# Moving the loads of the spike counts from SP's DMA queue to POOL's in the last stage of a gated attention layer

## The reference

```python
xn = layernorm(x)
# attention by pooling, 16 heads of 64
mixed_q = xn @ Wq + bq
mixed_k = xn @ Wk + bk
q_w = softmax((mixed_q @ Wqa + bqa) * scale, axis=tokens)
pooled_q = sum over tokens of q_w * mixed_q          # one row of 1024
mixed_qk = mixed_k * pooled_q
k_w = softmax((mixed_qk @ Wka + bka) * scale, axis=tokens)
pooled_k = sum over tokens of k_w * mixed_qk         # one row of 1024
s = (pooled_k * mixed_q) @ Wt + bt + mixed_q
# feed-forward with spikes
y = square(relu(xn @ W_fc.T)) @ W_proj.T             # hidden size 4096
cnt = number of spikes of y in 5 steps               # 0 to 5
out = x + s * silu(cnt / 5)
```

## Time and profile before

| what | value |
|---|---|
| median of 2 runs | 1622.05 us (1620.1 to 1624.01) |
| profiled execution | 1621.26 us |
| span of its slowest core (core 5) | 1619.6 us |
| spans of the eight cores | 1595.9 to 1619.6 us |
| granted TensorE clock, mean by core | 0.921 to 0.931 |
| busy: PE, DVE, ACT, POOL | 83%, 45%, 23%, 9% of the span |
| moved by DMA on this core | 174.19 MB, 108 GB/s |

### The profile page before, as it was taken

The page is one execution under the profiler, slowest core; times in us unless marked ns, Lnnn a source line. Parts: engine busy times, 40 slices in busy tenths (PEclk is TensorE's granted clock), DMA queues, the critical chain, the costliest instruction groups (busy, mean ns, idle before and its releaser), DMA issues.

```text
span 1619.6 us, 26631 instructions; the slowest of 8 cores (1595.9 to 1619.6 us)
## 1 busy us (share of the span) xinstructions
PE 1349.4 (83%) x8997; PEld 838.4 (52%) x8997; DVE 727.5 (45%) x1257; ACT 365.5 (23%) x804; POOL 149.9 (9%) x268
## 2 busy tenths in 40 slices
PE   1165599999999999999999999999999076379983
PEld 0032266666666666666666666666666032134431
DVE  3221136546464554645546465464645411244544
ACT  1323322313222131221313223132222000011221
POOL 1334400000000000000000000000022025120000
PEclk9976699999999999999999999999999575589997
DMA  6857701011010111101111010110013937647776
GB/s 184 249 170 243 244 28 60 34 66 45 36 60 33 53 47 47 60 31 55 46 47 59 21 60 34 66 59 21 34 59 101 318 117 217 226 136 235 235 248 219
DMA packets 66559, 174.19 MB, mean 108 GB/s; under 512 B 9671, under 2 KB 10071, under 8 KB 66410
## 3 DMA queue, kind: packets, MB, share of 16 engines
q1 hardware_dynamic: 34234, 77.90, 16.8%
q0 software_dynamic: 13824, 46.21, 8.3%
q10 hardware_dynamic: 18368, 48.37, 7.8%
HBM read 121.99 MB, written 50.46 MB: 106 GB/s over the span
## 4 chain that ended last, share of the span: by engine, by line
PE 69%; DMA 18%; DVE 5%; ACT 3%; issue 2%; SPq 2%; POOL 1%; DVEq 0%; ACTq 0%; POOLq 0%
PE PS L518 26%; PE PS L497 26%; PE PS L402 7%; DMA AM<-cnt_scratch 7%; DMA XF<-WfcT 2%; PE PS L681 2%; DMA XF<-WprojT 2%; DMA AB<-xtm_scratch 2%; PE PS L406 2%; PE PS L816 2%; PE PS L899 1%; SPq L633 1%; DMA OB<-WprojT 1%; DMA SCA<-xn_scratch 1%; ACT YS L527 1%
## 5 line engine op out<-in xcount | busy, mean ns | idle before, releaser
L497 PE MATMUL PS<-SCA,AB 128*128 128x256 bf16 x4096 | 539.9, 276 | 45.6 <-ACT RB L502 45.6
L518 PE MATMUL PS<-AB,AM 128*128 128x512 bf16 x2048 | 543.0, 385 | 6.3 <-ACT YS L527 4.7
L497 PEld LDWEIGHTS PS<-SCA,AB 128*128 128x128 bf16 x4096 | 403.3, 99 | 210.0 <-issue 57.0
L506 DVE TENSOR_TENSOR AM<-RB 128x256 bf16<-128x256 f32 x512 | 225.1, 440 | 554.4 <-PE PS L518 257.3
L502 ACT ACTIVATE RB<-PS 128x256 f32<-128x256 f32 x512 | 196.6, 384 | 761.8 <-PE PS L497 317.0
L518 PEld LDWEIGHTS PS<-AB,AM 128*128 128x128 bf16 x2048 | 189.1, 99 | 165.4 <-issue 26.3
L402 PE MATMUL PS<-SCA,AM 128*128 128x256 bf16 x1024 | 139.6, 280 | 49.7 <-DVE SCA L410 34.6
L552 DVE SCALAR_TENSOR_TENSOR AM<-YS,AM 128x1024 bf16<-128x1024 f32 x128 | 156.4, 1222 | 0.8
L402 PEld LDWEIGHTS PS<-SCA,AM 128*128 128x128 bf16 x1024 | 101.5, 100 | 67.0 <-issue 53.7
L278 POOL CAST AB<-OB 128x512 bf16<-128x512 f32 x55 | 35.9, 654 | 1039.2 <-PE PS L497 1001.3
L899 PE MATMUL PS<-AM,AB 128*128 128x512 bf16 x384 | 91.5, 392 | 3.2 <-DVE OB L926 1.9
(11 more groups left out here) (120 smaller groups left out, 694.9 us busy)
## 6 DMA issues: line engine op xcount, KB each, us to landing
XF<-x SPq DMA_DIRECT2D x64, 512.0 KB, 4.6
xn_scratch<-SCA ACTq DMA_DIRECT2D x16, 512.0 KB, 2.7
xtm_scratch<-SCA ACTq DMA_DIRECT2D x32, 256.0 KB, 3.2
mq_scratch<-SCA ACTq DMA_DIRECT2D x16, 512.0 KB, 2.7
cnt_scratch<-AM ACTq DMA_DIRECT2D x32, 256.0 KB, 3.2
AB<-xtm_scratch SPq DMA_DIRECT2D x32, 256.0 KB, 9.5
AM<-cnt_scratch SPq DMA_DIRECT2D x32, 256.0 KB, 5.2
out<-OB POOLq DMA_DIRECT2D x16, 512.0 KB, 6.3
```

The source lines that it names most:

```text
L497: pl.comp("tensor", lambda te, hb=hb, lt=lt, rh=rh, c=c: te.matmul(hb[:, 0:256], lt, rh, start=(c == 0), stop=(c == 7)), reads=a1keys(c * ...
L506: pl.comp("vector", lambda v, h2=h2, rr=rr: v.tensor_mul(h2, rr, rr), reads=[krr], writes=[("h2", g3)])
L518: pl.comp("tensor", lambda te, yb=yb, lt=lt, rh=rh, j=j: te.matmul(yb[:], lt, rh, start=(j == 0), stop=(j == 31)), reads=[kh2] + a2keys(j ...
```

## The change

`ld_cnt3` issues its DMA from POOL's stream in place of SP's. It has 32 calls: two ahead of the last loop, and one at the end of each of the loop's first 30 tiles. Slots, keys and semaphores are the same.

```diff
         def ld_cnt3(t):
             slot = AM[:, 10240 + (t % 2) * 1024: 10240 + (t % 2) * 1024 + 1024]
             alias = [("spk",)] if t % 2 == 0 else [("spk",), ("h2", 2), ("h2", 3)]
-            pl.dma("sync", f"cr{t % 2}",
+            pl.dma("gpsimd", f"cr{t % 2}",
                    lambda s, slot=slot, t=t: s.dma_start(slot, cnt_d[t]),
                    reads=[("cntd", t)], writes=[("cntr", t % 2)] + alias)
```

## The result

The changed kernel is slower by 0.8%: ratio to the kernel before 1.0082, with a 95% interval of 1.0056 to 1.0108. Of 1622 us that is 13 us, where the prediction had +10 and a range of 1614 to 1660. The median over all its runs is 1639.91 us, the profiled execution took 1636.4 us; its slowest core, core 1, has a span of 1634.5 us. Three of its executions took 1734 to 1824 us with four cores at a clock of 0.79 to 0.87 in place of 0.92, and ratios and intervals here leave such executions out for every kernel.

A forecast was written before the change was run, and what follows sets the result against it. Waits on count loads in the last loop, with neither TensorE nor DMA engines full, were taken to set 10.76 us a pair. +0.64 us over 15 pairs is +10 us: 1621.26 + 10 = 1631 us, range 1614 to 1660.

The forecast's parts named there:

- What bounds the kernel: Last loop: neither TensorE nor DMA is full; waits on count loads set 10.76 us a pair, through two nearly equal loops.
- The even loop as a whole: Last loop, even tiles: 7.2 us from addition to counts landed, plus 4.2, gives 11.4 us a pair against 10.76.
- The issue of the even counts: POOL, behind the even store: counts issued 1.21 us after the addition, against 0.55 on SP, 0.66 us later.
- The landing of the even counts: POOL's queue: store lands 7.1 us after the addition, counts 0.6 behind it at 7.7, less relief 7.2.
- the half microsecond of relief from sharing: SP's queue carries 256 KB less, 1.1 us; half of it, 0.5 us, is credited to POOL's queue.
- The odd load: Odd counts on POOL, nothing ahead: landing in 3.6 us is covered, in 5.2 makes the next even load 0.5 us late; put at nothing.
- The sum: Last loop: +0.64 us a pair over 15 pairs, +10 us, giving 1631 us.
- The early loads: Two count loads ahead of the last loop, on POOL behind mq loads: 21 us wait inside 35 us idle, put at nothing.
- A: Rival: the odd loop was what cost and gets shorter, no change or faster, 1619 or 1595 us; chance 0.18.
- B: Rival: POOL's queue gets the small share, even counts land late, over 2% slower, +47 us, 1668; chance 0.17.
- C: Rival: DMA bandwidth as a whole sets the pace, so the time stays at 1621 to 1623 us; chance 0.13.
- The signs: Profile after: count-load share not below 7%; wrong if additions under 10.6 us, odd landing last, or store doesn't delay counts.

The follow-up runs named there:

- store_sp_nokey: store_sp with no count load from tile 2 on waiting for the load before: ratio to the kernel before 1.0012 (0.9994 to 1.0029).
- nokey_sp: Kernel before, counts still on SP, without the shared key from tile 2 on: no interval, two of four times 1621.75 and 1629.02 us, against 1624.9.
- half_even: Changed kernel with even tiles' stores from POOL moving only 512 of 1024 columns: ratio to the kernel before 0.9998 (0.9982 to 1.0014).
- half_odd: Changed kernel with odd tiles' stores from ACT moving only half of their columns: ratio to the kernel before 1.0075 (1.0054 to 1.0096).
- odd_pool: Kernel before with only odd tiles' counts issued from POOL: no interval, two of four times 1621.05 and 1623.35 us, against 1622.05.
- even_pool: Kernel before with only even tiles' counts issued from POOL, odd ones from SP: ratio to the kernel before 1.0179 (1.0153 to 1.0206).
- nokey_pool: Changed kernel without the shared key from tile 2 on, so no count load waits for the one before: ratio to the kernel before 1.0192 (1.0161 to 1.0222).
- store_sp: Changed kernel with even stores issued from SP, even counts still waiting for the even addition: ratio to the kernel before 1.0003 (0.998 to 1.0026).

## Why the prediction was right

*What bounds the kernel.* Right as far as it went: loads with waits set the pace and not the engines' capacity. That two loops are nearly equal was read from the earlier trace rows, and store_sp_nokey and nokey_sp bear it out: without the chain the pace stays. "Most even loads go out right behind their x" holds for core 5 (8 of 14, tile 2's left out) and not for the chip: over the eight cores 48 of 112 do, and 73 start within 0.12 us of the odd landing, some of them both. The pair that was read, 9.7 us from x to x, is one of the short ones.

*The even loop as a whole.* Averages of the eight cores, even tiles, us:

| | before | after | half_even | half_odd |
|---|---|---|---|---|
| end of the addition to the start of the counts | 0.93 | 1.54 | 1.62 | 1.29 |
| start to landing | 5.49 | 5.54 | 4.63 | 5.79 |
| landing to the end of the next even addition | 4.36 | 4.21 | 4.23 | 4.21 |
| sum | 10.78 | 11.30 | 10.48 | 11.28 |
| even loads at the least start (of 112) | 48 | 51 | 36 | 90 |
| even loads that start right at the odd landing (of 112) | 73 | 51 | 69 | 6 |

(A load counts as at the least start up to 0.65 us after the addition before the change and up to 1.2 after it; as right at the odd landing up to 0.12 us behind it from SP and 0.56 from POOL.) Forecast were 7.2 + 4.2 = 11.4 against 10.76; measured 7.1 + 4.2 = 11.3 against 10.8. So the pair is nearly as forecast and half_odd nearly is the forecast's pure even loop. The 7.1 is a sum of two misses that cancel, which is luck: the start comes 0.3 us later than the 1.21, since nearly half of the even loads wait for the odd one, and the landing is 0.5 us shorter than the 6.0. Against the kernel before, the added time is the later start; the landing behind a store is what the landing behind x was.

*The issue of the even counts.* Forecast 1.21 us after the addition; measured 1.12 in the slow pair and 1.5 in the last part (1599.84 after an addition that ended at 1598.32). Right in the first; in the second the counts waited for the odd load, which landed at 1599.32, and started 0.52 us after it, as every load of that part did.

*The landing of the even counts.* Forecast 6.0 us after their issue (7.2 less 1.21); 6.0 is the mean on core 1, 5.5 that of the eight cores (5.1 to 6.0). On core 1 the number is right and its parts are not. Two stretches make it, 6.4 to 8.0 and 4.1 to 5.5. The store ahead landed sooner than the 6.4 that I took over (5.4; there is less beside it in SP's queue, which was not tested as the reason), and the counts landed up to 3.1 us behind it in the slow stretch, 2.1 in the pair shown; outside it 0.5 to 1.0, close to the 0.6 taken from the x pair. For the half microsecond of relief from sharing half_odd gives no support: with 256 KB a pair less in ACT's queue the even counts landed no sooner (5.8 us). SP's own queue was not tested.

*The odd load, put at nothing.* Wrong in the quieter part. I chose 3.6 us from a quieter stretch; it landed in 4.8, and the next even load waited for it. From 1566 us on, ten loads in a row on core 1 start 0.52 to 0.55 us after the landing before, so there the chain of loads is the pace. The text had this case at 0.5 us a pair for a landing of 5.2. The direct cost of POOL there is two starts of 0.48 us a pair, where SP needed 0.04 each.

*The sum.* +0.64 us a pair was forecast. Core 1 has +0.81 a pair against the 10.76 of core 5, the mean of the cores 2 x (5.63 - 5.37) = +0.52, which is 31 x 0.26 = 8 us of loop. By the ratio it is 13 us, three more than forecast. The slowest core counts, and the cores lie further apart in pace (5.49 to 5.80 us a tile, before 5.32 to 5.46); how much of the 13 that makes was not taken apart further.

*The early loads, put at nothing.* Right. POOL on core 1 ahead of the loop, which answers to the earlier trace rows:

```profile
1369.92 0.54 POOL L759 DMA_DIRECT2D AM<-cnt_scratch  x1
1393.97 0.54 POOL L759 DMA_DIRECT2D AM<-cnt_scratch  x1 [23.50 <-DMA AM<-cnt_scratch]
1405.15 2.10 POOL L861 DMA_DIRECT2D SCA<-mq_scratch  x4 [10.64 <-PE PS L670]
```

The wait for the first landing was 23.5 us, near the 21 of the text, and the 4 loads of mq were issued when they had been.

*The rivals.* A (the odd loop gets shorter and pays) fell, though its premise was sound: before the change 73 of 112 even loads started right at the odd landing. The odd landing did shrink, from 4.95 to 4.21 us over the eight cores, but each link of the chain now holds POOL's 0.5 us, and odd_pool, with 4.60, shows no gain. B had its mechanism half right: in the slow stretch the even counts land 8.55 us after the addition (1505.45 + 7.43 against 1504.33), the next ones 9.07, about the 8.7 from which B was to decide, but only in stretches (8 of the 120 even loads of the chip pass it), and nothing showed that half shares of a turn cause it; 2 KB against 4 KB rows were not tested. even_pool and nokey_pool, at 1.8 and 1.9%, are what the kernel looks like when this stretch is nearly all there is. C fell with the first result. The Trainium skill gives DMAs from GpSimd a first byte at about 1 us and those from SP and ACT one at about 0.6 in "DMA: Bandwidth & Descriptors", section Specifications. The difference of 0.4 us, an estimate from these two, was not separated by any run; store_sp, all of whose counts come from POOL, lands them in 4.9 us where SP's took 5.2 in another company.

*The signs.* The share of AM<-cnt_scratch "not lower than 7%" was a bad sign to name: it fell to 4%, and out<-OB is not in the list. "If the odd landing comes last" was named as a sign of being wrong, and it came true in part: on core 1 from 1566 us on, and for 51 of 112 even loads of the chip. The other two did not: pairs of additions stayed above 10.6 on average (11.3), and half_even shows that the store ahead delays the counts.

What stays open: why some stretches and some cores fall into the slow pattern and others not (on core 3, 5.54 us a tile, most loads of either parity land in 4.5 to 5.5).

## What to carry to other kernels

A DMA moved to an idle engine takes its place in that engine's order and in its queue: ask what is issued just before it, what that waits for, and how many bytes it puts ahead. A small load that others wait for does not belong behind a large store, even if its own queue looks empty. Where two bounds stand at one height, here a false wait between two slots and a late issue, remove both before judging either: one alone gave nothing (1.0006 and 1.0012) or a loss (1.0192), both together 0.6% on SP and 1.1% on POOL, and with the store's move 1.4%.

## What the runs showed that I had not expected

- POOL begins a DMA about 0.5 us after what it waited for, SP 0.04 to 0.07 us after. In a chain of dependent loads this is paid in each link.
- Spacing can be worth more than freedom: nokey_pool, with a wait less than the changed kernel, is slower (1.0192 against 1.0082); its loads start together, and the even ones, which set the pace, land in 6.9 us in place of 5.5.
- Which queue holds the bytes matters more than how many there are: 256 KB less a pair in POOL's queue took the ratio from 1.0082 to 0.9998, in ACT's to 1.0075, which is inside the changed kernel's interval.
- A median of landings hid the loss: it fell from 5.2 to 4.8 us while the kernel got slower. The fall is all in the odd loads (4.95 to 4.21 us), and the even ones stayed at 5.5 and started later.
